# Three-layer CIN on one core: W1's last tiles are loaded third, and products of the next chunks stand between the rounds that make A

## The reference

```python
X0 = inputs.reshape(-1, 32, 64)            # 64 samples x 32 fields x 64 dimensions
Xi = X0
for W, b in ((W1, b1), (W2, b2), (W3, b3)):        # each 128 outputs
    Xi = einsum('bhd,bmd,ohm->bod', X0, Xi, W.reshape(128, 32, m)) + b
    pools.append(Xi.sum(axis=-1))
return concat(pools) @ fc_W.T + fc_b
```

## Time and profile before

| | |
|---|---|
| median of 3 runs | 81.17 us (81.09 to 81.17) |
| the profiled execution | 81.42 us, its span 79.6 us |
| granted clock of TensorE | 1.00 |
| PE busy | 73.1 us (92%), 372 records |
| PEld | 52.3 us (66%) |
| POOL | 48.7 us (61%) |
| DVE | 45.9 us (58%) |
| ACT | 34.9 us (44%) |
| DMA | 12.01 MB |

### The profile page before, as it was taken

One profiled execution on the slowest core, in us unless ns is written; L12 is line 12 of the kernel. 1 busy time (PEld: TensorE's weight loads), 2 busy tenths in 40 slices (PEclk: granted clock), 3 DMA queues, 4 the chain that ended last, 5 costly groups with the idle time before them and its releaser, 6 DMA issues.

```text
span 79.6 us, 1146 instructions
## 1 busy us (share of the span) xinstructions
PE 73.1 (92%) x372; PEld 52.3 (66%) x372; DVE 45.9 (58%) x45; ACT 34.9 (44%) x51; POOL 48.7 (61%) x48
## 2 busy tenths in 40 slices
PE   4999499978994999999999999999999999999970
PEld 1345176843440677888888888888888888886840
DVE  1067699786959999790649969992003003203541
ACT  1833997649955859975645520570300300000000
POOL 4999844999992693929166989619946004162400
DMA  0898999999985361714999700000000000000000
GB/s 26 243 366 280 355 377 350 382 389 384 376 288 138 96 175 44 215 34 94 404 381 315 301 8 0 4 0 0 0 0 0 0 0 0 8 0 0 0 0 0
DMA packets 7529, 12.01 MB, mean 151 GB/s; under 512 B 835, under 2 KB 3971, under 8 KB 7267
## 3 DMA queue, kind: packets, MB, share of 16 engines
q1 hardware_dynamic: 6915, 11.16, 41.0%
q10 hardware_dynamic: 608, 0.77, 3.1%
HBM read 10.88 MB, written 1.05 MB: 150 GB/s over the span
## 4 chain that ended last, share of the span: by engine, by line
PE 70%; DMA 10%; POOL 5%; DVE 4%; SPq 4%; issue 4%; ACT 1%; DVEq 0%; POOLq 0%
PE a_ps L586 28%; PE x_ps L586 25%; DMA x_in<-xl 10%; PE z_ps L580 4%; DVE r_in L475 3%; POOL feat L267 3%; PE a_ps L641 2%; PE a_ps L679 2%; PE a_ps L640 2%; PE x_ps L614 2%; SPq L196 2%; POOL xs L260 2%; PE x_ps L758 1%; SPq L184 1%; SPq L210 1%
## 5 line engine op out<-in xcount | busy, mean ns | idle before, releaser
L267 POOL TENSOR_TENSOR feat<-r_in,feat 128x1024 fp32r<-128x1024 f32 x8 | 19.5, 2442 | 6.3 <-ACT feat L358 5.9
L586 PE MATMUL x_ps<-feat,w_hi 128*128 128x512 f32 x64 | 19.2, 395 | 0.0
L586 PE MATMUL a_ps<-feat,a_hi 128*128 128x512 f32 x64 | 16.2, 395 | 0.0
L508 DVE SCALAR_TENSOR_TENSOR x<-a_ps,vec,x 128x512 f32<-128x512 f32 x7 | 5.2, 748 | 16.7 <-PE a_ps L641 16.6
L274 POOL TENSOR_TENSOR x<-x 128x512 f32<-128x512 f32 x6 | 7.8, 1293 | 10.9 <-DVE x L508 10.7
L586 PEld LDWEIGHTS x_ps<-feat,w_hi 128*128 128x128 f32 x64 | 11.9, 189 | 3.4 <-issue 0.8
L586 PEld LDWEIGHTS a_ps<-feat,a_hi 128*128 128x128 f32 x64 | 11.9, 188 | 2.7
L260 POOL TENSOR_TENSOR xs<-x_in,xs 32x512 fp32r<-32x512 f32 x7 | 9.8, 1395 | 5.7 <-ACT xs L358 5.4
L358 ACT ACTIVATE feat<-z_ps 128x1024 fp32r<-128x1024 f32 x8 | 8.2, 1026 | 6.5 <-DVE z_ps L475 6.5
L482 DVE TENSOR_TENSOR feat<-z_ps,feat 128x1024 fp32r<-128x1024 f32 x8 | 9.7, 1219 | 1.5 <-ACT feat L358 1.5
L358 ACT ACTIVATE feat<-r_in 128x1024 fp32r<-128x1024 f32 x8 | 8.5, 1058 | 3.0 <-DVE r_in L475 2.9
(11 more groups left out here) (76 smaller groups left out, 73.4 us busy)
## 6 DMA issues: line engine op xcount, KB each, us to landing
w_sb<-w SPq DMA_DIRECT2D x9, 512.0 KB, 8.7
x_in<-xl SPq DMA_DIRECT2D x8, 256.0 KB, 7.3
r_in<-xr SPq DMA_DIRECT2D x2, 1024.0 KB, 7.0
a_by_fields<-at_sb SPq DMA_DIRECT2D x8, 96.0 KB, 2.0
x<-x ACTq DMA_DIRECT2D x1, 512.0 KB, 4.6
x<-x SPq DMA_DIRECT2D x1, 512.0 KB, 5.9
w_sb<-w SPq DMA_DIRECT2D x1, 256.0 KB, 10.2
a_by_fields<-at_sb SPq DMA_DIRECT2D x4, 64.0 KB, 1.8
```

Of the source, the lines that this page charges most:

```text
L267: nc.gpsimd.tensor_tensor(feat[:, c, 1, of_half(1), :], z_of(c, 1), feat[:, c, 0, of_half(1), :].bitcast(f32), ALU.subtract).then_inc(lo_d ...
L508: nc.vector.scalar_tensor_tensor(out=x1[:, c, :], in0=a_ps[:, c % 2, :], scalar=vec[:, 3:4], in1=x1[:, c, :], op0=ALU.add, op1=ALU.mult).t ...
L586: nc.tensor.matmul(bank, weights[:, k, :], feat[:, c, part, k, :], start=(start and k == 0), stop=False)
```

## The change

On SP, W1's last tiles are loaded third, ahead of inputs 2 and 3; inputs 2 and 3 stand ahead of all of W3. On ACT and DVE, the work on W1's last tiles moves forward to chunk 1 and 2, `hi(0, 0)` stands ahead of W1's rounding, and `save_x1` of every chunk to 5 moves forward. On PE, tail 0 stands ahead of A's first round, and x1 parts of chunks 1, 2 and 3 stand between the rounds and between the picks of later chunks; `x1_product(5)` stands ahead of `a_product(0)`, `a_product(4)` ahead of `x1_product(7)`. On DVE, the products with x1 (`product`) of chunks 0, 1 and 2 stand inside the work on chunks 6 and 7. Chunk 5 is still picked by PE. No operation is added or removed.

```diff
 SP
             load_x(1)
+            sp.dma_start(w1_sb[:, :, EVEN:, :], w1[:, :, EVEN:, :]).then_inc(w1_rest_in, 16)
+            load_x(2)
+            load_x(3)
             load_w3(0)
             load_w3(1)
-            load_x(2)
             load_w3(2)
             load_w3(3)
-            load_x(3)
...
-            sp.dma_start(w1_sb[:, :, EVEN:, :], w1[:, :, EVEN:, :]).then_inc(w1_rest_in, 16)
 DVE
             lo(0)
+            rest_sum()
             dve.wait_ge(w_hi_done, 1)
             main_lo(w1_sb[:, 0, :, :], w1_hi, w1_lo, w_lo_done)
             chunk(1)
-            chunk(2)
-            mult(3, 0)
-            rest_sum()
-            mult(3, 1)
-            lo(3)
+            mult(2, 0)
             dve.wait_ge(w_hi_done, 2)
             rest_lo(w1_sb[:, 0, :, :], w1_hi, w_lo_done)
+            mult(2, 1)
+            lo(2)
+            chunk(3)
...
-            chunk(6)
+            mult(6, 0)
             product(0)
+            mult(6, 1)
             product(1)
-            chunk(7)
-            for c in range(2, CHUNKS - 1):
+            lo(6)
+            mult(7, 0)
+            mult(7, 1)
+            product(2)
+            lo(7)
+            for c in range(3, CHUNKS - 1):
 ACT (first part)
             split_x(1)
+            hi(0, 0)
             act.wait_ge(w_sum, 1)
             copy(w1_hi[:, 0:TILES, :], w1_sb[:, 0, 0:TILES, :]).then_inc(w_hi_done, 1)
-            hi(0, 0)
             hi(0, 1)
+            split_x(2)
             save_zz(0)
-            split_x(2)
+            act.wait_ge(w_rest_sum, 1)
+            copy(w1_hi[:, EVEN:, :], w1_sb[:, 0, EVEN:, :]).then_inc(w_hi_done, 1)
             hi(1, 0)
+            split_x(3)
             hi(1, 1)
-            split_x(3)
...
+            hi(2, 0)
             act.wait_ge(v_ready, 1)
 PE
+            pick_right(2, 0)
+            x1_hi(1, 0)
             v_part(2)
-            pick_right(2, 0)
+            v_part(3)
             pick_right(2, 1)
-            v_part(3)
+            x1_lo(0, 1)
             nc.tensor.transpose(v_ps, vt_sb[:, :], ident[:, :]).then_inc(v_ready, 1)
-            x1_lo(0, 1)
-            pick_right(3, 0)
+            x1_tail(0)
+            x1_lo(1, 0)
             a_round(0)
             a_round(1)
-            x1_hi(1, 0)
+            pick_right(3, 0)
+            x1_main(1, 1)
             pick_right(3, 1)
+            x1_low_weights(1, 1)
+            x1_lo(1, 1)
+            x1_tail(1)
+            x1_main(2, 0)
             a_round(2)
             a_round(3)
             pick_right(4, 0)
-            x1_lo(1, 0)
             pick_right(4, 1)
-            x1_hi(1, 1)
-            x1_lo(1, 1)
-            x1_tail(0)
-            x1_tail(1)
+            x1_low_weights(2, 0)
+            x1_lo(2, 0)
             spread16(1)
-            pick_right(5, 0)
-            x1_hi(2, 0)
-            x1_lo(2, 0)
-            pick_right(5, 1)
             x1_hi(2, 1)
             x1_lo(2, 1)
+            x1_hi(3, 0)
+            pick_right(5, 0)
             x1_tail(2)
-            x1_product(3)
+            x1_lo(3, 0)
+            x1_hi(3, 1)
+            pick_right(5, 1)
+            x1_lo(3, 1)
+            x1_tail(3)
             x1_product(4)
+            x1_product(5)
```

More of the change, by code:

```diff
@@ L408, in _ @@
             copy(v_st[:, H + 8:H + 15], v_by_field[:, 1, 0:7]).then_inc(v_saved, 1)
-            hi(2, 0)
+            act.wait_ge(vec_in, 16)
+            save_x1(0)
+            hi(2, 1)
             split_x(4)
-            hi(2, 1)
             save_a(0)
@@ L414, in _ @@
             hi(3, 0)
-            act.wait_ge(w_rest_sum, 1)
-            copy(w1_hi[:, EVEN:, :], w1_sb[:, 0, EVEN:, :]).then_inc(w_hi_done, 1)
-            split_x(5)
+            save_x1(1)
             save_a(2)
             save_a(3)
+            split_x(5)
             hi(3, 1)
             hi(4, 0)
-            act.wait_ge(vec_in, 16)
-            save_x1(0)
+            save_zz(1)
             hi(4, 1)
-            save_x1(1)
-            save_zz(1)
             act.wait_ge(zeros_done, ZEROS)
@@ L432, in _ @@
                     scratch.tensor, (TILES * j + k) * M, [[(EXT + 1) * M, H], [1, (TILES - k) * M]])).then_inc(f_main_in, 16)
+            save_x1(2)
             hi(5, 0)
@@ L437, in _ @@
                 [P, H, 4])).then_inc(v_saved, 1)
-            save_x1(2)
+            save_x1(3)
             act.wait_ge(f_sum, 1)
             copy(a_hi[:, 0:TILES, :], f1[:, 0:TILES, :]).then_inc(a_hi_done, 1)
-            save_x1(3)
             act.wait_ge(f_sum, 2)
@@ L447, in _ @@
             copy(q_sb[:, :], q_ps).then_inc(q_saved, 1)
+            save_x1(5)
             hi(6, 0)
@@ L452, in _ @@
             hi(7, 1)
-            save_x1(5)
             save_x1(6)
@@ L736, in _ @@
             a_product(1)
-            x1_product(5)
             a_product(2)
@@ L740, in _ @@
             a_product(3)
+            a_product(4)
             x1_product(7)
-            for c in range(4, CHUNKS - 1):
+            for c in range(5, CHUNKS - 1):
                 a_product(c)
```

## The result

The changed kernel takes 80.12 us (80.08 to 80.34, 4 runs) where the one before takes 81.17: a ratio of 0.9875, interval 0.9858 to 0.9893. It is faster, by 1.05 us and not by the 3.0 forecast, and 0.12 us above the range. Its profiled execution took 80.34 us, span 78.5; that run is some 0.25 us longer than the others from its start on, as W1's main tiles landed later (POOL's sum of them begins at 7.14, in a profiled run of 80.11 us at 6.88). PE is busy 73.3 us (93%), DVE 47.3, POOL 49.5, ACT 34.6, the granted clock is 1.00.

A forecast was written before the change was run, and what follows sets the result against it. PE bounds the kernel, with 3.3 us of holes from 13.97 to 40.28; chunk 5's product would end at 40.1 instead of 43.26, gain 3.15, less 0.15 for waits: 3.0, so 78.2 us, range 77.7 to 80.0.

The forecast's parts named there:

- the 3.0 forecast: Whole kernel: gain of 3.15 us less 0.15 for further waits, bringing the median to 78.2 us.
- the range: Whole kernel's time: 77.7 to 80.0 us, taking in the first two rivals and holding 0.87.
- the order of `rest_lo` and `lo(1)`: DVE and POOL, chunk 1: `rest_lo` gets SBUF at 17.1, done 17.5; `lo(1)` moves to 17.5 to 19.9.
- the prediction's walk: PE's new list from 13.97, laid out at 0.229 us a matmul, each supplier checked for being in time; chunk 5's product ends 40.1.
- The rival with chance 0.20: At `rest_lo`, DVE asks after POOL began `lo(1)`; ready at 20.0, PE loses 1.7 at tail 0: 79.9 us; chance 0.20.
- The ceiling of 3.3 us: PE from 13.97 to 40.28: 26.31 us less 23.0 of work leaves 3.3 us of holes, the most to gain.
- my count of work: PE from 13.97 to chunk 4's tail: matmuls 17.2, `v_part` 1.94, rounds 3.74, transpose 0.1, sum 23.0 us; chunk 5's product 2.98.
- the 0.15 that I had put in for unknown waits: PE's tight list: 0.15 us for a few more waits where a supplier is in time by 0.2 or less.
- the old wait at the pick of chunk 4: PE at 25.96 in the kernel before: 1.16 us, released by chunk 3's second multiplication, queued behind `rest_sum`; gone after the change.
- the race at `main_lo`: DVE asks for SBUF 0.2 us before POOL's split of input 2; if lost, 79.2 us; chance 0.07.
- A: A's last `save_a` doesn't move; last splits end 39.98, `a_product(0)` starts 40.2 and takes the last at 43; slack some 3 us.
- The later W3 and W2: Loads of W3 and W2 come 0.7 to 1.4 us later than before, yet in time for `v_part` and A's rounds.

The follow-up runs named there:

- the repeat: The changed kernel run once more with nothing altered, on the same chip as the kernel where POOL waits for `rest_lo`: 80.11, 80.09, 80.00, 78.88, 80.12 and 80.21 us.
- the first experiment: The changed kernel with `rest_lo` on DVE ahead of `mult(2, 0)` and not behind it: 78.98 us, ratio 0.9738 to the kernel before.
- the last experiment: The changed kernel with `x1_product(5)` back behind `a_product(1)`: 82.07 us; with `save_x1(5)` on ACT also back behind `hi(7, 1)`: 80.92 us.
- loads and `rest_sum` alone: The kernel before with the new order of loads and, on DVE, `rest_sum` behind `lo(0)`, nothing else: 80.15 us, ratio 0.9886.
- the one in which POOL gives way: The changed kernel with one wait more on POOL: `lo(1)` waits until `rest_lo` is done; DVE's and PE's lists unchanged: 79.03 us, ratio 0.9751.
- the loads alone: The kernel before with only the order of the loads changed: 12 runs, 79.97, 79.99, 80.32, 80.48 and eight from 81.05 to 81.19; median 81.07 us.

## Why the prediction was wrong

- *The failed step* is the order of `rest_lo` and `lo(1)`: "which asks for SBUF at 16.85 while POOL splits, and gets it at 17.1, ahead of `lo(1)`". In the changed kernel's trace DVE asks at 17.37 and POOL begins at 17.18. This run is 0.29 us later than the prediction's walk from the start (its `v_part` at 14.26, not 13.97), DVE and POOL alike. The profiled run of the repeat has its `v_part` at 13.97, so it can be laid on the walk: 17.08 against 16.90. The forecast had DVE 0.35 us ahead, it was 0.18 behind, and the 0.53 are small errors: DVE is 0.23 late, as I took 1.9 us from the pick of chunk 2 to the request (0.75 from pick to multiplication, though the earlier trace rows had 0.85, and 1.15 from there on, where it is 1.26), and it is 2.10 (14.98 to 17.08); POOL is 0.30 early, as I let its split of input 2 start at 12.0, held by `main_lo`, and it started at 11.69. Price: 80.12 - 78.98 = 1.14 us shown by moving DVE's instruction, 80.12 - 79.03 = 1.09 by holding POOL. The rival with chance 0.20 had the mechanism and priced it at 1.7, as it had POOL end its low part later and PE reach tail 0 earlier (at 18.3 from a start at 13.97; in the first experiment at 18.52 from 13.85). That its 79.9 lies within 0.2 of the measured time is partly luck: its price is 0.6 too high, and the 78.2 that it starts from is 0.8 too low.
- *The ceiling of 3.3 us was mis-sized.* "Named waits and short gaps together" were taken as holes that can be closed. In the first experiment PE has no wait from 13.85 to 40.51 + 0.23 = 40.74: 26.89 us, against 23.0 + 2.98 = 25.98 by my count of work. So 0.9 us are neither work by my prices nor holes. There are five blocks of f32 matmuls in that stretch (two of `v_part`, the transpose, two of rounds), and the time lies beside them: by starts, the matmuls between and behind them take 0.21, 0.12, 0.19, 0.20 and 0.22 us more than 0.229 each (14.86 to 16.44, 17.45 to 18.49, 18.52 to 19.40, 21.27 to 24.45, 26.32 to 40.74; of the last, 62 matmuls long, 0.12 is in its first four). The blocks themselves take what I gave them. The kernel before has five as well. What could be won was 3.3 - 0.9 = 2.4, and the first experiment won 81.11 - 78.98 = 2.13 by the medians, 2.54 between the profiled runs.
- Together: 1.14 + 0.9, less the 0.15 that I had put in for unknown waits, is 1.9, and 80.12 - 78.2 is 1.92.
- *Right:* the old wait at the pick of chunk 4 was `rest_sum` held by POOL after a late transfer, in two parts; PE has no other wait over 0.3 us behind 14 us, but for the 0.44 at the very end that the kernel before has too; W1's last tiles land at 8.8 as forecast (issued at 2.54, landed 6.3 us later); the race at `main_lo` is won (11.42 before POOL's 11.79), and `rest_sum` and `main_lo` take 0.61 and 0.68.
- *A* moved although I said it would not: its last `save_a` ends at 28.49, its last split at 41.97 + 0.55 = 42.52; with the race won, in the first experiment, they end at 27.03 and 41.06, still later than 26.63 and 40.0. It is hidden all the same, by chunk 5's product; it would not be without it, as the last experiment shows.
- *The later W3 and W2* cost nothing: no row of `v_part` or a round waits for a transfer.
- *What the rest of the change is worth*, the new order on PE with what goes with it on ACT and DVE: nothing as it stands, as loads and `rest_sum` alone give 80.15. With the race won it is 80.15 - 78.98 = 1.17. The waits at the transpose and at a pick that loads and `rest_sum` leave (0.49 and 0.31 by the rows, 1.1 by starts) are gone in the first experiment, where x1's parts stand; PE's part was not tried apart from ACT's and DVE's.

The fastest kernels are the first experiment and the one in which POOL gives way, 78.98 and 79.03 us, both faster than the kernel before and the changed one.

## What to carry to other kernels

Two instructions that shut each other out are a race between two engines' lists, and its outcome can be a step of a microsecond, as here. A forecast must put the two starts side by side, and where they are no further apart than the forecast can err (here 0.35 us of margin and 0.53 of error), make the order certain: move the short one to where the long one can't have begun, or let the long one wait for it. And count as a hole only what a row names as a wait; the short gaps beside blocks of another kind stayed when the order changed.

## What the runs showed of the hardware

- A DVE instruction that reads two SBUF operands, begun 0.04 us ahead of POOL's, takes 0.42 us (`rest_sum`, with the loads alone; POOL 2.63 instead of 2.39); begun 0.18 us behind it, 2.48 (`rest_lo`, 0.42 by itself). Where POOL was first, DVE's read ended 0.27 to 0.29 us after POOL's instruction: 24.68 after 24.41 before the change, 19.85 after 19.56 in the changed kernel, 41.08 after 40.80 in the last experiment. The Trainium skill's SBUF — State Buffer, "Who interferes with whom", has it that issue order, not the kind of instruction, decides who blocks. The traces here agree: the same `rest_lo` took 0.42 or 2.48 us by who was first.
- One program had two times with nothing changed: 79.97 and 81.1 us in one kernel, 80.1 and once 78.88 in another. Each was traced on one side only; that the race parts them is shown by the kernels without it, none of whose runs fell into the slower group.
- PE loses some 0.09 us going from fp32r products to small f32 ones of 32 output rows, 0.12 going back and 0.1 within the block: 0.35 us a block by the times. Whether the type or the fewer output rows costs it is open.
